# A graph network kernel: node order turned round, five early sums spread over tiles 7 to 24, and every source one-hot made by VectorE

## The reference

```
dst = minimum((3125 * uniform(100000) ** 2.0).astype(int32), 99999)   # then sorted
# layer 0: message sum, then a GRU cell
msg      = h[src] @ W_msg.T + b_msg + edge_embed[type]
messages = segment_sum(msg, dst)
x = layernorm(x + gru(messages, h))
# layer 1: two mean-aggregation layers
h = relu(x @ w_self1 + mean_agg(x) @ w_neigh1 + b1)
x = layernorm(x + h @ w_self2 + mean_agg(h) @ w_neigh2 + b2)
```

## Time and profile before

| | |
|---|---|
| time, median of 3 runs | 761.78 us (761.57 to 763.35) |
| the profiled execution | 763.88 us, of which 762.1 us span |
| mean granted TensorE clock | 0.979 of full speed |
| PE busy | 666.3 us (87%) |
| DVE busy | 466.6 us (61%) |
| ACT busy | 249.8 us (33%) |
| POOL busy | 165.7 us (22%) |
| tile loop | about 14 us to 395 us |
| end of the tile loop to the GRU stage | about 395 us to 414.6 us |

### The profile page before, as it was taken

How to read it: one execution, slowest core, us unless ns; L and a number is a source line. 1 busy time by engine, 2 the same in 40 slices (tenths; PEclk the granted TensorE clock), 3 DMA queues, 4 the chain that set the end, 5 groups by cost and what they waited for, 6 DMA issues and landing times.

```text
span 762.1 us, 14806 instructions
## 1 busy us (share of the span) xinstructions
PE 666.3 (87%) x3067; PEld 311.8 (41%) x3067; DVE 466.6 (61%) x1469; ACT 249.8 (33%) x501; POOL 165.7 (22%) x340
## 2 busy tenths in 40 slices
PE   2777767777889999999989999958999999999995
PEld 0222222222333443444434544423555456666663
DVE  7999969999899889888883357551010010044434
ACT  3665654222332433443364245531111221100000
POOL 2565524333222222222220012230100111100000
PEclk9999979999999999999999999978999999999998
DMA  5000000000000000000011001001100111211210
GB/s 155 0 0 0 0 1 1 0 0 1 0 1 0 1 1 1 0 1 1 1 49 33 16 28 55 16 29 30 42 28 14 41 41 30 77 54 42 70 31 15
DMA packets 29433, 17.28 MB, mean 23 GB/s; under 512 B 1841, under 2 KB 28223, under 8 KB 29400
## 3 DMA queue, kind: packets, MB, share of 16 engines
q1 hardware_dynamic: 29400, 16.82, 7.5%
HBM read 10.38 MB, written 6.44 MB: 22 GB/s over the span
## 4 chain that ended last, share of the span: by engine, by line
PE 62%; DVE 20%; issue 8%; DVEq 6%; ACT 2%; DMA 1%; POOL 0%; SPq 0%; ACTq 0%
PE PS L888 11%; PE PS L959 11%; DVE S L602 11%; PE PS L849 11%; PE PS L1197 11%; DVE D L596 4%; PE PS L1126 3%; PE PS L1020 2%; DVEq L602 2%; PE PS L1161 2%; DVEq L623 2%; PE PS L1114 1%; PE PS L1115 1%; PE PS L993 1%; PE PS L994 1%
## 5 line engine op out<-in xcount | busy, mean ns | idle before, releaser
L888 PE MATMUL PS<-S,D 128*128 128x449 bf16 x786 | 221.3, 365 | 54.5 <-DVE S L602 49.7
L602 DVE TENSOR_SCALAR S<-iota_h,src_col,src_w 128x440 bf16<-128x440 f16 x747 | 249.6, 387 | 0.0
L455 POOL COPY S<-T 128x27 bf16 (+1 forms) x264 | 111.9, 425 | 234.3 <-PE PS L888 219.7
L888 PEld LDWEIGHTS PS<-S,D 128*128 128x128 bf16 x786 | 75.8, 96 | 196.1 <-DVE S L602 166.1
L1240 ACT ACTIVATE AT<-digits 128x1152 uint8 (+5 forms) x75 | 77.1, 1029 | 174.9 <-DVE digits L591 174.9
L596 DVE TENSOR_TENSOR D<-iota_t,dst 128x384 bf16<-128x384 f16 x262 | 91.5, 349 | 29.4 <-PE PS L888 29.2
L849 PE MATMUL PS<-AT,xp 128*128 128x512 bf16 x375 | 89.3, 379 | 0.8 <-ACT Cn L1228 0.8
L959 PE MATMUL PS<-AT,x1p 128*128 (+2 forms) x450 | 86.8, 353 | 0.0
L1197 PE MATMUL PS<-xp,AT 128*128 128x384 bf16 (+1 forms) x525 | 85.6, 326 | 0.0
L1197 PEld LDWEIGHTS PS<-xp,AT 128*128 (+2 forms) x525 | 51.5, 98 | 33.9 <-issue 0.3
L959 PEld LDWEIGHTS PS<-AT,x1p 128*128 128x128 bf16 x450 | 39.5, 99 | 44.1 <-issue 2.4
(11 more groups left out here) (162 smaller groups left out, 621.7 us busy)
## 6 DMA issues: line engine op xcount, KB each, us to landing
slot<-x_rows SPq DMA_DIRECT2D x12, 256.0 KB, 2.9
xstage<-x SPq DMA_DIRECT2D x6, 256.0 KB, 5.2
x_rows<-slot SPq DMA_DIRECT2D x6, 256.0 KB, 2.2
y_rows<-slot SPq DMA_DIRECT2D x6, 256.0 KB, 2.2
res_rows<-slot SPq DMA_DIRECT2D x6, 256.0 KB, 2.2
slot<-res_rows SPq DMA_DIRECT2D x6, 256.0 KB, 2.8
out_rows<-slot SPq DMA_DIRECT2D x6, 256.0 KB, 2.2
slot<-xT SPq DMA_DIRECT2D x3, 256.0 KB, 2.5
```

The source lines that it names most:

```text
L455: g.tensor_copy(S[:, where:where + V, SPAN:WIDE], T[:, :, ds(c0 + where, V)].rearrange("p k c -> p c k")).then_inc(sem("types_placed"), 1)
L602: v.tensor_scalar(S[:, u, 0:SPAN], iota_h[:, :], src_col[:, ds(c0 + u, 1)], src_w[:, ds(c0 + u, 1)], ALU.is_equal, ALU.mult).then_inc(sem( ...
L888: mm(PS[:, par, 0:WIDE], ring[:, u, :], S[:, u, 0:WIDE], start=opens and u == 0, stop=last).then_inc(sem("tiles_summed" if last else "item ...
```

## The change

1. **Node order.** x, src, dst and type come in reversed order, and the kernel computes with node 3124 - n. ScalarE turns the sources round (`src_i`), one more activation at the start which VectorE waits for; the destinations are turned in the instruction that already centred them. The tiles with the most edges now come last. `more` is 2, then 3 eight times, 4, 3, 4, 3, 4, 5, 4, 5, 5, 5, 6, 7, 8, 9, 15, 17: 130 batches, since the last tile no longer gets at least two batches beyond the end. The least number of batches is 2 in tiles 0 to 20 and 4 in tiles 21 to 24.
2. **Help dropped.** ScalarE's `last_rows` is gone. VectorE makes all six source one-hots of every batch. (`helped` is always None.)
3. **Early sums.** Groups 0 to 4 (EARLY = 5, one more PSUM bank) are laid out in one row of 125 steps. EARLY_PLAN gives each tile its steps: none in tiles 0 to 6, then 4 to 10; 120 in the loop, 5 behind it. In tiles 21 to 24 (now `is_dense`) a tile's steps stand in five pieces: two more after the first and the second batch.
4. **Digits.** The last tiles take digits sooner, so that only tile 24's remain behind the loop; `turn_tile(23)` stands inside tile 24. In the tail the five remaining steps (15 matmuls) stand ahead of the last turn.

```diff
-EARLY = 4
-EARLY_BANKS = (2, 3, 5, 6)
-EARLY_CUTS = (0, 7, 13, 19, TILES)
+EARLY = 5
+EARLY_BANKS = (2, 3, 5, 6, 7)
+EARLY_PLAN = (0,) * 7 + (4, 4, 5, 4, 5, 4, 5, 7, 5, 7, 7, 7, 8, 10, 9, 9, 10, 10)
...
+        def taken_at(t):
+            return {TILES - 4: ((TILES - 7,), (), ()), TILES - 3: ((TILES - 6,), (), (TILES - 5,)),
+                    TILES - 2: ((), (), (TILES - 4,)), TILES - 1: ((), (TILES - 3,), (TILES - 2,))}[t]
+
         def is_dense(t):
-            return isinstance(t, int) and t < LAG
+            return isinstance(t, int) and t >= WIDE_TILES
...
             def early_piece(t, n):
-                q, r = divmod(t - LAG - 4, 4)
-                if 0 <= q < EARLY:
-                    j0, j1 = EARLY_CUTS[r:r + 2]
-                    early_sum(q, j0 + (j1 - j0) * n // LEAST, j0 + (j1 - j0) * (n + 1) // LEAST)
+                pieces = PIECES + 2 if is_dense(t) else PIECES
+                n0, steps = EARLY_BEGIN[t], EARLY_PLAN[t]
+                early_steps(n0 + steps * n // pieces, n0 + steps * (n + 1) // pieces)
...
+                if is_dense(t):
+                    for i in (1, 2):
+                        one_pass(first + t + i, first + i, D, None)
+                        early_piece(t, i)
+                    if t == TILES - 1:
+                        turn_tile(t - 1)
+                    with pe.Fori(3, more) as i:
+                        one_pass(first + t + i, first + i, D, None)
+                    early_piece(t, 3)
+                    one_pass(first + t + more, first + more, D, None, closes=True, between_halves=lambda: early_piece(t, 4))
...
-            turn_tile(TILES - 2)
-
-            pe.wait_ge(sem("packed_out"), TILES)
-            early_sum(EARLY, 0, 8)
+            early_steps(EARLY_BEGIN[TILES], EARLY * TILES)
             turn_tile(TILES - 1)
-            early_sum(EARLY, 8, 20)
             pe.wait_ge(sem("verdict_set"), 1)
-            mm(PS[0:1, 7, 0:1], ones[:, 0:1], verdict[:, :], start=True, stop=True).then_inc(sem("verdict_sum"), 1)
-            early_sum(EARLY, 20, TILES)
+            mm(PS[0:1, 0, 0:1], ones[:, 0:1], verdict[:, :], start=True, stop=True).then_inc(sem("verdict_sum"), 1)
...
+            act.wait_ge(sem("src_in"), 32)
+            a.activation(src_i[:, :], raw_src[:, :], ACT.Copy, scale=-1.0, bias=float(N - 1)).then_inc(sem("src_turned"), 1)
...
             for t in range(LAG):
-                first, more = tile_entry(act, t)
-                last_rows(t, first + 1, first + 1)
                 tile_steps(t, (t - 1) % 2)
                 if t == 2:
                     for c in range(NC + 1):
                         x_mid(c)
-                with act.Fori(2, more + 1) as i:
-                    last_rows(t, first + i, first + i)
```

More of the change, by code:

```diff
@@ L30 @@
 V = U // 2
-LEAST = 3
+PIECES = 3
+WIDE_TILES = 21
+LEAST = 2
+LEAST_WIDE = 4
 BATCHES = -(-CHUNKS // U)
-assert BATCHES + LEAST < 1 << 10 and LEAST * TILES < BATCHES
+assert BATCHES < 1 << 10 and LEAST * WIDE_TILES + LEAST_WIDE * (TILES - WIDE_TILES) < BATCHES
 LAG = 3
@@ L57 @@
 CUTS = (0, 9, 18, TILES)
-EARLY = 4
-EARLY_BANKS = (2, 3, 5, 6)
-EARLY_CUTS = (0, 7, 13, 19, TILES)
+EARLY = 5
+EARLY_BANKS = (2, 3, 5, 6, 7)
+EARLY_PLAN = (0,) * 7 + (4, 4, 5, 4, 5, 4, 5, 7, 5, 7, 7, 7, 8, 10, 9, 9, 10, 10)
+EARLY_BEGIN = tuple(sum(EARLY_PLAN[:t]) for t in range(TILES + 1))
+assert EARLY_BEGIN[TILES] <= EARLY * TILES
 SCRATCH = 2048
@@ L107, in graph_kernel @@
     dst2 = place(r, "dst2", [P, CP, 2], fp16)
+    src_wn = place(r, "src_wn", [P, BATCHES + 2], fp32)
     assert r[0] <= A_at + part_bytes
@@ L120, in graph_kernel @@
     last_i = place(r, "last_i", [TILES, CHUNKS], i32)
+    src_i = place(r, "src_i", [P, CP], i32)
     src_high = place(r, "src_high", [P, CP], i32)
@@ L158, in graph_kernel @@
     plain = sb("plain", [1, 32], fp32)
+    least = sb("least", [1, 32], fp32)
     words = sb("words", [1, 32], fp32)
@@ L177, in graph_kernel @@
     src_w = place(r, "src_w", [P, CP], fp32)
+    apart = place(r, "apart", [P, SPAN], bf16)
     assert r[0] <= Z_at + 15 * F * 4
@@ L571, in _ @@
+            v.tensor_scalar(src_low[:, :], src_i[:, :], P - 1, None, ALU.bitwise_and)
+            then(v.tensor_scalar(src_digit[:, :], src_i[:, :], 7, DIGITS - 1, ALU.logical_shift_right, ALU.bitwise_and))
             v.tensor_tensor(src_col[:, :], src_high[:, :], src_low[:, :], ALU.add)
@@ L622, in edge_rows @@
                 between(0)
[L623 to L626, removed]
+                if is_dense(t):
+                    one_hots(t, first + 1, par, False)
+                    between(1)
+                    one_hots(t, first + 2, par, False)
+                    with dve.Fori(3, more) as i:
+                        one_hots(t, first + i, par, False)
+                    between(2)
+                    one_hots(t, first + more, par, False)
+                else:
+                    with dve.Fori(1, more) as i:
+                        one_hots(t, first + i, par, False)
+                    between(1)
+                    one_hots(t, first + more, par, False, lambda: between(2))
             def x_rest(c):
@@ L669, in _ @@
             dve.wait_ge(sem("verdict_sum"), 1)
-            then(v.tensor_scalar(flag[:, 0:1], PS[0:1, 7, 0:1], float(E), None, ALU.not_equal))
+            then(v.tensor_scalar(flag[:, 0:1], PS[0:1, 0, 0:1], float(E), None, ALU.not_equal))
             v.tensor_copy(flag_i[:, 0:1], flag[:, 0:1]).then_inc(sem("flag_set"), 1)
```

117 lines of the change are left out of this document (63 added, 54 removed).

## The result

The changed kernel takes 768.96 us, median of 7 runs (766.36 to 770.13), beside 763.31 us for the kernel before in 7 runs on the same chip (761.57 to 765.23). The ratio is 1.0069, with a 95% interval of 1.0053 to 1.0085. It is slower by 0.7%. The profiled execution took 770.13 us with a span of 768.3, against 763.88 and 762.1: 6.2 us.

A forecast was written before the change was run, and what follows sets the result against it. VectorE and TensorE were taken to wait for each other through a one-batch ring, VectorE the busier, with a tail chain behind. Loop +13.0, last half batch +0.6, tail -8.7 and clock +1.7 gave +6.6: 768.4 us, range 761 to 773.

The forecast's parts named there:

- rival A: Whole kernel: the lost help outweighs the shorter tail, 764.1 to 773 us; the forecast itself, chance 0.60.
- Help dropped: Tile loop: VectorE makes one more source one-hot in each of 45 formerly helped batches, 0.30 us each, +13.5 us.
- Start: Kernel start: ScalarE's turning round of the sources delays VectorE, +0.3 us, bounds 0 and 0.85 + 0.2.
- the split of x: Opening tiles: the wait stays, but ScalarE's helped one-hot ahead of packed_out(1) is gone, -0.7 us.
- One batch less and two digit takings more: Tile loop: 130 batches for 131, -2.4 us; 24 takings of digits for 22 at 0.95 us each, +1.9 us.
- Tile starts: VectorE's waits at tile boundaries: 29.6 us against 29.2, spreading early sums hardly helps; +0.4 us, bounds -13 and +6.
- Loop +13.0, last half batch +0.6: Loop ends 13.0 us later in sum; TensorE's last half batch then begins 0.1 us behind VectorE, not 0.55 ahead, +0.6.
- Tail: Last half batch to GRU stage: shorter chain, 11.7 us for 20.4, -8.7 us, bounds -6.7 and -9.3.
- Clock: GRU stage's first matmuls: TensorE's clock falls in the nearly idle tail, +1.7 us, bounds 0 and 3.5.
- Rival B: Tile loop: spread early sums stop VectorE's waiting; waits below 20.7 us, time below 759.5 us; chance 0.12.
- Rival C: Whole kernel: terms fall kindly, clock costs nothing, tail gains 9.3; +4.3 us, 761 to 764 us; chance 0.15.
- Rival D: Sparse opening tiles: TensorE's clock is down to half, +5 us over six tiles, 773 us; chance 0.13.

The follow-up runs named there:

- e1: Kernel before with only ScalarE's help dropped, VectorE making all six source one-hots; 775.41 us, ratio 1.0143.
- e5: Changed kernel with the same early steps per tile in four pieces instead of three in tiles 7 to 20, one behind the first batch; 760.88 us, ratio 0.9956.
- e7: Changed kernel with unused matmuls added in tiles 1 and 2 to hold TensorE's clock; 768.51 us, ratio 1.0044.
- e8: Kernel before with only a fourth piece of early sums behind the first batch in tiles 7 to 22; 745.77 us, ratio 0.9761.
- e2: Changed kernel with the last turn moved ahead of nine of the last fifteen early matmuls; 768.56 us, ratio 1.0062.
- e3: Changed kernel with 16 unused matmuls behind the last turn and 4 behind the verdict's matmul; 765.91 us, ratio 1.0032.
- e6: Changed kernel with earlier last turn, fewer unused tail matmuls (8 for 16), help in tiles 23 and 24, four pieces, unused opening matmuls; 750.3 us, ratio 0.9829.
- e4: Changed kernel with ScalarE's help given back for 24 batches of tiles 23 and 24; 764.62 us, ratio 1.0008.

## Why the prediction was right, point by point

The forecast was 768.4 us, the time is 768.96, and rival A is what happened. That the two lie 0.6 us apart is partly luck: the forecast was +6.6 on a median of 761.78, measured was +5.65 on one of 763.31. The steps in their order:

- **Help dropped, +13.5.** Right: e1 shows +12.36 us in the loop, which is 13.5 with 1.0 us less waiting. The unhelped half batch costs 1.18 us at either end of the kernel.
- **Start, +0.3; the split of x, -0.7.** VectorE's first one-hot of tile 0 stands at 14.53 for 14.40, and at 14.53 to 15.08 in the seven profiles of the turned order for 14.28 to 14.40 in the three of the old one: +0.1 to +0.8. The wait for the split was 5.00 for 5.49 us, -0.49, but 5.40 or 5.41 in e1 to e5, so of the 0.7 only 0.1 is what the dropped one-hot gives; the rest of it goes with the clock (3.88 in e7). One batch less and two digit takings more, -2.4 and +1.9, weren't tried apart.
- **Tile starts, +0.4.** Measured 28.0 - 29.2 = -1.2. The classes hold: five steps 1.07 for 0.8, six 1.5 to 1.7 for 1.4 (1.3 at tile 24), seven 2.0 to 2.1 for 2.1, nine 3.4 for 3.5; most too cheap were the eight at tile 21, 3.58 for 2.8. Too dear were the pieces behind batches 1 and 2 of tiles 21 to 24, 0.5 for 2.4 us (one wait of 0.52 in tile 24 is all there is), tiles 1 to 6 with 2.0 for 3.0, and the wait of 0.7 us for digits in tile 24, which didn't come. The argument behind the term, that spreading by tiles doesn't help while the pieces stay at the boundary, is borne out by e5 and e8: the same number of steps with a fourth piece in mid-tile takes 9.3 and 15.0 us off the wait.
- **Loop +13.0, last half batch +0.6.** VectorE's last one-hot ends at 405.45 for 394.66, +10.8, and the half batch on TensorE stands 0.9 us further back: +11.7 for +13.6. Of the 2.2 us missing in the loop the tile starts are 1.6; with e1's price in place of 13.5 the terms would come nearer, but its 1.0 us of waiting is partly the same wait. The last 0.6 can't be settled, because executions differ by more (below).
- **Tail, -8.7.** Measured 20.44 to 11.14, -9.3, at the bound that the prediction gave; the flag was there at R + 9.15 for 9.5, and from there to the transposes it took 2.0 us for 2.2. e2 shows that nine of the matmuls ahead of the turn had still been on the chain.
- **Clock, +1.7 with bounds 0 and 3.5: the term that was mis-sized.** It was taken from the pair of the earlier trace rows, 27 matmuls behind a pause, and measured 4.0 us, above the upper bound. e3 shows that the mechanism is right, by taking it away. The pair was too short a sample: in it the half clock lasts for part of 7.51 us, here it stays at 0.50 from 414 to 426, on fp32 matmuls that show 1.91 us a pair for 1.02. The forms of the matmuls alone don't make it last: in e6 the same ones, behind a pause of 4.05 us, are back at 1.00 from 403 on, 3 us after they began at 400.02. What does make it last was not tried.

So two errors of 2 us, the loop priced 1.9 too high and the clock 2.3 too low, offset each other, and the median came out nearer than its parts. Rival B is refuted for this change, but e8 shows that its state exists: the wait of 14.2 us is below the 20.7 us from which it decides. Rival C had the right fall of the tail, but not the clock at no cost. Rival D has a true core that is small: between 30 and 54 us the clock is down to 0.50 for long stretches and costs 1.7 to 2.8 us up to tile 4 (e7), while the other opening tiles run at 1.00 with waits under 0.5 us, so its price for six tiles didn't arise. The Trainium skill ("TensorE: Matmul & The Clock Gate", section "HAM oscillation — how this bites in real kernels") says that each wait between bursts may lead to a cold start of the next; the runs here agree in the tail (12.58 against 8.55 us) and at the split of x.

## What to carry to other kernels

Where two engines wait for each other through a ring of one batch, other work put on the less busy one should be counted by where it stands together, not by tile or by total: here four steps around a tile's boundary cost nothing and each further one 0.5 to 0.8 us, about its full 0.65, and one piece moved into the tile took the wait from 29.2 to 14.2 us with the same work (e8). Before an engine's help is dropped, price it on the engine that bounds: 0.30 us a batch came to twice what the whole change lost. And a chain made short by moving matmuls out of it leaves TensorE idle ahead of the next stage; count the half clock that follows against the gain, or fill the pause.

## What the runs showed of the hardware

A pause of TensorE can cost more than its length: 4.0 us at the GRU stage in the kernel after, 1.7 us at pass 2 in most profiles. How long the half clock lasts behind it isn't fixed. The same matmuls of the GRU stage began at 416.96, 416.39, 412.16, 408.97 and 415.47 us in the kernel after, e2, e4, e5 and e7, and windows of 1 us show full clock again at about 426.1, 424.6, 420.6, 417.8 and 426.0: 8 to 11 us later, and the first late sum 12.1 to 13.2 us behind the transposes. In e6 it was 3 us and 9.89. What was gained ahead of such a stretch was partly lost again in e7, and was kept in e2. The first 27 matmuls of pass 2 are the same in all kernels here; they take 5.83 us in e3, e6 and e8, and 7.46 to 7.72 in the seven others' profiles.

The same instructions take different times in the opening tiles: the kernel after and e2 to e5 are alike up to tile 4, and VectorE reaches it at 59.90 us in the first and at 60.97 to 61.54 in the others, with TensorE's clock changing level at different moments. With the clock held, in e6 and e7, it is 58.40 and 58.33. Most of the 4 us between the fastest and the slowest of a kernel's runs may come from this and from pass 2; no run separates them. Effects under 1 us were therefore read from one stretch of a trace and not from times.
